# Uneven chunks in the preparation of a two-network graph kernel, and the record store cleared in pieces

## The reference, cut to what matters

```
for l in range(6):
    W = (ssp(edge_attr @ mlp_w1[l] + mlp_b1[l]) @ mlp_w2[l] + mlp_b2[l]) * C[:, None]
    msg = (h @ conv_w1[l])[src] * W
    agg = segment_sum(msg, dst)                    # dst is sorted
    h = h + ssp(agg @ conv_w2[l] + conv_b2[l]) @ lin_w[l] + lin_b[l]
x = layernorm(x + h)
# then three layers of a second network: agg = segment_sum(h[src], dst), two products, layernorm
```

## Time and profile before

| | |
|---|---|
| median of three runs | 5893.71 us (5890.15 to 5894.4) |
| the profiled execution, own time | 5894.77 us |
| its span in the profile | 5893.1 us |
| preparation, start to the first edge product | 0 to about 1070 us |
| six layers of the first network | about 1070 to 5617 us |
| busy: PE, POOL, DVE, ACT | 4903.4, 4011.3, 3560.8, 2777.2 us |

### The profile page before, as it was taken

How to read it: one execution, slowest core, us unless ns; L and a number is a source line. 1 busy time by engine, 2 the same in 40 slices (tenths; PEclk the granted TensorE clock), 3 DMA queues, 4 the chain that set the end, 5 groups by cost and what they waited for, 6 DMA issues and landing times.

```text
span 5893.1 us, 130525 instructions
## 1 busy us (share of the span) xinstructions
PE 4903.4 (83%) x33026; PEld 3993.5 (68%) x33041; DVE 3560.8 (60%) x10645; ACT 2777.2 (47%) x4801; POOL 4011.3 (68%) x5030
## 2 busy tenths in 40 slices
PE   1036446899999999999998999999999999999999
PEld 0035446777777777777777777877778777777644
DVE  8412224576666766667676666766667667666522
ACT  0012223455555555555555555555555555555422
POOL 4777773577776777767777677776777767777500
PEclk5567778999999999999999999999999999999999
DMA  8258667533333333333333333434333343333200
GB/s 344 77 167 277 213 218 242 165 123 117 119 119 119 124 119 118 119 120 123 120 122 116 119 120 119 124 117 120 121 119 122 117 122 123 118 121 118 90 2 10
DMA packets 431082, 778.19 MB, mean 132 GB/s; under 512 B 55099, under 2 KB 115973, under 8 KB 427349
## 3 DMA queue, kind: packets, MB, share of 16 engines
q1 hardware_dynamic: 388108, 728.55, 38.9%
q0 software_dynamic: 20640, 34.39, 1.8%
q10 hardware_dynamic: 21928, 11.64, 0.7%
HBM read 605.57 MB, written 168.79 MB: 131 GB/s over the span
## 4 chain that ended last, share of the span: by engine, by line
PE 57%; issue 13%; POOL 11%; DVE 9%; DVEq 6%; DMA 1%; ACT 1%; SPq 1%; ACTq 0%; POOLq 0%
PE ps_a L706 14%; PE ps_a L686 12%; PE ps_w L696 12%; PE ps_h L787 12%; POOL permuted L571 11%; DVE aggT L1456 6%; DVEq L333 3%; PE ps_pair L905 3%; DVEq L1456 1%; DVE src_hot L1495 1%; DVEq L427 1%; DVE hid L1585 1%; DVEq L1509 1%; PE ps_pair L720 1%; DVE counts L1509 1%
## 5 line engine op out<-in xcount | busy, mean ns | idle before, releaser
L589 POOL TENSOR_SCALAR phot<-pwin_now,prel_now,pcut_now 128x128 f32<-128x128 f32 x4224 | 3298.7, 796 | 1021.2 <-PE ps_a L706 985.6
L1456 DVE TENSOR_TENSOR aggT<-aggT,ps_a 128x128 f32 x4224 | 1212.8, 287 | 888.0 <-issue 367.0
L686 PEld LDWEIGHTS ps_a<-hi_mid,buffers 128*128 128x128 f32 x8448 | 1127.7, 195 | 575.8 <-issue 575.1
L706 PE MATMUL ps_a<-phot,ex_msg 128*128 128x128 f32 x8448 | 1204.7, 287 | 276.7 <-DVE aggT L1456 276.0
L706 PEld LDWEIGHTS ps_a<-phot,ex_msg 128*128 128x128 f32 x8448 | 1053.9, 196 | 342.0 <-issue 330.5
L1075 ACT ACTIVATE xc<-ps_h 128x512 f32<-128x512 f32 x1056 | 630.4, 597 | 1278.3 <-PE ps_h L787 1265.1
L686 PE MATMUL ps_a<-hi_mid,buffers 128*128 x8448 | 1143.2, 279 | 30.7 <-ACT hid L1035 27.9
L787 PE MATMUL ps_h<-buffers,edge_w 112*128 112x512 f32 x2112 | 1136.7, 621 | 7.7 <-DVE hid L1585 7.7
L696 PE MATMUL ps_w<-edge_w,hid 128*128 128x128 f32 x8448 | 1120.3, 276 | 0.0
L696 PEld LDWEIGHTS ps_w<-edge_w,hid 128*128 128x128 f32 x8448 | 1034.4, 193 | 0.0
L1585 DVE SCALAR_TENSOR_TENSOR hid<-xc,ps_h 128x512 f32<-128x512 f32 x1056 | 722.8, 684 | 335.7 <-PE ps_w L696 267.9
(11 more groups left out here) (236 smaller groups left out, 2875.6 us busy)
## 6 DMA issues: line engine op xcount, KB each, us to landing
buffers<-src_select SPq DMA_DIRECT2D x1056, 256.0 KB, 2.8
buffers<-attr_permuted SPq DMA_DIRECT2D x1056, 224.0 KB, 2.8
hid<-permuted SPq DMA_DIRECT2D x176, 208.0 KB, 4.3
counts<-in_rec SPq DMA_DIRECT2D x19, 1404.0 KB, 9.9
permuted<-aggT SPq DMA_DIRECT2D x26, 944.0 KB, 26.8
src_select<-ex_msg SPq DMA_DIRECT2D x88, 256.0 KB, 4.8
src_select<-buffers SPq DMA_DIRECT2D x88, 256.0 KB
attr_permuted<-ex_msg SPq DMA_DIRECT2D x88, 224.0 KB, 3.6
```

The source lines that it names most:

```text
L589: op = pool.tensor_scalar(phot[:, u % 2, t, :], pwin_now[:, :], prel_now[:, u * TPG + t:u * TPG + t + 1], pcut_now[:, u * TPG + t:u * TPG ...
L686: mm = pe.matmul(ps_g[:, t * F:(t + 1) * F], select[:, u % AS, t * P:(t + 1) * P], table[:, bass.ds(starts[t], F)], start=True, stop=True)
L706: mm = pe.matmul(ps_a[:, t * PWIN:(t + 1) * PWIN], msg[:, u % 2, t * F:(t + 1) * F], phot[:, u % 2, t, :], start=True, stop=True)
L1456: dve.tensor_tensor(window, window, ps_a[:, t * PWIN:(t + 1) * PWIN], ALU.add).then_inc(part_added[t] if t < TPG - 1 else add_done[u % M], 1)
```

## The change

The chunks become 68, 60 and 48 groups, that is 253, 221 and 171 tiles. The parts are then 31 to 32, 27 to 28 and 21 to 22 tiles, against 26 to 28 before. A clear has 16 pieces, not 13. The clears of chunks 1 and 2 are no longer issued right after the first three record loads: chunk 1's pieces go out three or four at a time behind the record loads r = 3 to 7, chunk 2's two at a time behind r = 8 to 15, ahead of the groups turned there. `EARLY_AT` moves two of its three entries one iteration later, because chunk 2 now begins at group 128 and not at 117.

```diff
-CHUNK_GROUPS = [59, 58, 59]
+CHUNK_GROUPS = [68, 60, 48]
-CLEARS = 13
+CLEARS = 16
-EARLY_AT = [5, 8, 9]
+EARLY_AT = [5, 9, 10]
...
-            def clear(k):
+            def clear(k, pieces=range(CLEARS)):
...
-                for c in range(CLEARS):
+                for c in pieces:
...
             clear(0)
             for r in range(RING):
                 load_records(r)
-            for k in range(1, CHUNKS):
-                clear(k)
             wait_table(sp, 16 * EARLY, 16)
             for r in range(RING, CHUNKS * PARTS):
                 load_records(r)
+                k, p = r // PARTS, r % PARTS
+                if k == 0:
+                    clear(1, range((p - RING) * CLEARS // (PARTS - RING), (p + 1 - RING) * CLEARS // (PARTS - RING)))
+                elif k + 1 < CHUNKS:
+                    clear(k + 1, range(p * CLEARS // PARTS, (p + 1) * CLEARS // PARTS))
                 for g in turned_after(r):
                     turn_group(g)
```

## The result

The changed kernel took 5875.55 us (median of 8 runs, 5872.59 to 5879.65), the one before, measured again beside it, 5893.2 us. The ratio is 0.997, with a 95% interval of 0.9959 to 0.9981: 17.7 us faster. The forecast was 5873.9. The profiled execution took 5872.65, 22.1 us less than that of before.

The account below looks back on a forecast made before the run. POOL's scatter was taken to bound 63 to 913 us, then turning the last chunk's groups. Terms -24.3 + 6.7 - 2.5 + 0.3 = -19.8 us took the median from 5893.7 to 5873.9 us; 8-in-10 range 5867 to 5888.

Parts of the forecast that it names:

- The last chunk: Turning after the last scatter: 48 groups instead of 59, 11 fewer at 2.21 us each, -24.3 us (bounds -22.5 to -25).
- over 2.4 us for each group of the last stage: Sign that the forecast is wrong: turning after the last scatter takes over 2.4 us for each group.
- The first chunk: Preparation before POOL's first scatter: `find_places(0)` grows from 217 to 253 tiles, scatter starts +6.7 us later (+5.5 to +8).
- the 7 us that I had worked out: Start: first clear and loads need 62 us, DVE ends at 68.6 us, so cover is 7 us.
- The surplus of the scatter: POOL's scatter issues lengthened beside DVE's work on places: 34.6 us surplus changes by -2.5 us net (0 to -5).
- Waits for records: POOL ahead of part 17, chunk 2's first: records ready at +27.0, needed at +26.7, stall 0.3 us (0 to 6).
- Clears and node steps: Moved clears hidden beside the scatter, node steps one iteration later in the layers: nothing, +-3 us for loop alignment and measurement.
- Rival 1: Record loads for part 17 and one or two beside it come 3 to 8 us late; around 5885 us; chance 0.22.
- Rival 2: Chunk 1's scatter: clears delay every part's records; gain gone if a pair costs over 9.9 us, 5922 at 14; chance 0.08.
- their cover is the 1.6 us for each part that POOL has in hand: Chunk 1's scatter: part takes 33.5 us against POOL's 35.1, hiding chunk 2's clears; uncovered, two pieces cost 4.9 us.
- Rival 3: Scatter's 34.6 us surplus stays, long issues not depending on DVE's operation length; -17.3, 5876.4 us; chance 0.11.
- Rival 4: Last stage bound by POOL's memsets, not by groups, so the end is not shortened; 5898 us; chance 0.02.

## Why the prediction was right, and where it was off

**The last chunk.** -24.3 us predicted, 141.9 - 118.3 = 23.6 measured. The rate of the later groups was the right one to take: 23.6/11 is 2.15 us for a group. One of the prediction's signs of being wrong, over 2.4 us for each group of the last stage, was badly set: over the whole stage it is 118.3/48 = 2.46, but by the same count it was 141.9/59 = 2.41 before, since both hold the slow start.

**The first chunk.** +6.7 predicted, 63.06 to 69.81 is +6.75. DVE set the start, as the step had it. The first clear was in time, with more cover than the 7 us that I had worked out: by the trace it was complete at 50.6 us, and DVE's signal came at 68.8.

**The surplus of the scatter.** -2.5 predicted. The scatter's busy time is now 652.7 us, so the surplus over 645 x 0.96 went from 34.6 to 33.5: -1.1. The five long issues that belong to chunk 2 did shrink as predicted, by 3.5 us (15.7 against 19.2, four fifths). The six before them grew by 3.0 instead of 1.2; why is told below.

**Waits for records.** +0.3 predicted, 2.8 measured, within the bounds. The mechanism and the place (part 17) were right, three terms were a little off: load 17 was issued 18.2 us after chunk 2 began and not 17.4; it landed after 10 us as before, although it is 22% smaller (the 0.9 us that I took off is not there); and POOL went on 0.8 us after DVE's last fill operation. A part took SP 32.5 us in chunk 1, against 33.5 predicted.

**Clears and node steps.** Taken at nothing. That clears beside turned groups cost nothing on a 5.9 ms chip is shown by the kernel with all clears in chunk 0, which has the same total. That taking them away from the start gains nothing is read from the trace of before: no issue of the scatter behind the first waited over 0.31 us, and the first waited for DVE. The node steps changed nothing by the kernel that has them alone, though on the other kind of chip.

**The sum.** -19.8 predicted, -15.0 in the trace up to the end of turning, -17.7 in the medians. The surplus and the wait, 1.4 and 2.5 us, are most of the missing 4.8. So the median came within 1.7 us of the forecast partly by luck: 2.7 of its 17.7 us are not from the preparation, and no run explains them. The range too was added up wrongly: the bad ends of the terms (-22.5, +8, 0, +6, +5) give -3.5 us and not about -7.

**The rivals.** Rival 1 (loads give part back) came true in small. Rival 2 (slower, record loads late in every part) did not happen where the prediction was made, and did on the other chips: there the clears cost 38.8 us in chunk 1's scatter, and the change loses 34 us in all. The price that I had set for it, a pair that costs over 9.9 us, was not the way it came: the pair costs 4.9 us there, but nothing hides it, since the part is already longer than POOL's share. The step that would not have held is "their cover is the 1.6 us for each part that POOL has in hand": it is read from one execution on one chip, and on the others a part took 50 us against POOL's 34 already before the change, so that nothing was in hand. The trace that I had could not show this. Rival 3 (the surplus stays) gave -17.3 us, close to the median, but its mechanism is out, since chunk 2's long issues did shrink. Rival 4 is out too: the last stage did get shorter.

## What to carry to other kernels

Cost a moved DMA by the stretch that it moves into and ask what hides it there: the same clear pieces were free beside a scatter alone, free beside a nearly full stretch with slack, and cost 4.9 us a pair where that slack was gone. Where work is pipelined over chunks of a bound engine and really hidden beside it, make the last chunk small, since it is drained in the open (where turning was not hidden, the sizes alone gave a ratio of 0.9992); the limits are the start and the first part of the smaller chunk, which arrives sooner than its records. When engines stand idle beside each other, look whether the data had been moved before you blame the DMAs: here they had, and the wait was for another engine's signal. And measure a change that leans on work hidden beside POOL's scatter on more than one chip.

## What the runs showed of the hardware that I had not expected

**How well other work overlaps with POOL's indirect DMAs differed from chip to chip.** Alone, each ran alike: the scatter 1.27 us a tile, turned groups 2.2 us each, the first clears and loads above 400 GB/s. Beside each other the DMA engines were busy for 0.89 to 0.92 at about 300 GB/s in two sets of runs, and for 0.46 to 0.54 at 150 to 173 GB/s on three chips. There SP's data were moved in time, but PE's hand-over of a turned group was up to 40 us late while POOL was scattering; in the last stage ACT began 0.04 us after PE's last product, as on the other chips. The cause was not found; no kernel here scatters beside PE without SP's DMAs or the other way round. Of the chips that are noted none was seen in both ways, and the chip of the first set is not noted; so that this goes with the chip rests on the repeats within each set of runs alone.

**A scatter issue that meets a long DVE operation on two inputs in SBUF ends about 0.83 us after it.** In the changed kernel, DVE and POOL at two moments:

```profile
81.42 5.00 DVE L1255 TENSOR_TENSOR buffers<-counts 128x4641 bf16<-128x4641 f32 x1 [0.15 <-DVE counts L1342]
...
81.48 5.76 POOL L574 DMA_INDIRECT permuted<-counts  x1 [0.30 <-issue]
...
179.51 3.90 DVE L1255 TENSOR_TENSOR buffers<-counts 128x3591 bf16<-128x3591 f32 x1 [0.15 <-DVE counts L1342]
...
180.31 3.94 POOL L574 DMA_INDIRECT permuted<-counts  x1 [0.31 <-issue]
```

DVE ends at 86.42 and 183.41, POOL at 87.24 and 184.25; before, 209.60 and 210.42. Ten of the eleven meetings of each trace end so, and only the first of all is later, by 1.18 us. So the surplus of one meeting is the operation's length less how far into it the issue falls, which may be anything up to 1.27 us. That phase is what the step on the surplus had left out: in the first six meetings DVE's operations grew by 1.3 us in sum, as expected, but POOL's issues fell earlier into them, by 1.7 us in sum. The long reduction (7.5 us, line 1260) and the scans that read PSUM held up nothing.
